# Merging the routing and the expert parts of a small transformer's kernel into one unrolled part

## The chip, the cores and the metric

The kernel runs on one core of a Trainium2 chip. The metric is the device time of one execution in microseconds (us), lower is better. Engines are named as in the profile: PE is TensorE (PEld its weight loads), DVE is VectorE, ACT is ScalarE, POOL is GpSimd, SP is SyncE, which issues the DMAs.

## What is computed

Two layers over x of shape 4 x 1024 x 128 in float32. Each layer is attention and a feed-forward part, each with a layer norm and a modulation (shift, scale, gate) by batch. Only the first layer's feed-forward part matters here. It is a mixture of 16 experts with 64 hidden columns each, and one shared expert:

```python
mod = (silu(L0_c) @ L0_wmod).reshape(4, 6, 1, -1)      # sa, ca, ga, sb, cb, gb
gb = (2 * (gb >= 0) - 1) * maximum(abs(gb), 0.25)
h = layernorm(x) * (1 + cb) + sb
scores = sigmoid(h @ gate_w.T)
# biased = scores + gate_bias; the 2 best of 4 groups of experts stay, of them the 4 best experts;
# weight[token, expert] = scores where chosen, else 0
y = sum_e weight[:, e] * (silu(h @ w1[e].T) * (h @ w3[e].T)) @ w2[e].T
y = y + (silu(h @ ws1.T) * (h @ ws3.T)) @ ws2.T
x = x + gb * y
```

After it come the second layer (windowed attention, then a two-layer local transformer) and the output; the change leaves them alone.

## The kernel before

The token vectors stay in SBUF as X, 32 tiles of 128 tokens, 8 tiles a batch. The program is a sequence of blocks with a barrier between them; in a block each engine runs its own list, tied by semaphores.

**setup** loads constants and computes the modulation. Rows that are multiplied along the free axis are spread over all partitions in rowB (five of them); the gate of the experts, gbT, is kept as a column.

**linear_attention** takes two batches at a time. Each half has two steps of normalisation (ln_stats and ln_apply on DVE, ln_rstd on POOL between them), transposes on PE, the q and v product, a softmax of q on DVE and ACT, and at the end the output products (L463) and the residual on DVE. POOL does only ln_rstd here.

**moe** has two blocks. The first is the routing, a loop over the four batches. A batch is normalised and transposed; ACT writes hT and its rounded copy h_hi, POOL the rest h_lo; PE makes the logits (L565); ACT the exponentials; DVE turns them into scores and compares them pair by pair (wins, gwins, beaten: L629 to L639), makes the weights comb (L662) and splits them into three bfloat16 parts, which PE transposes and ACT stores in combT. The normalisation of the next batch lies between (L166). At the end POOL splits w1 and w3 into two parts each (L555, L556).

The second block is the experts. The 1024 hidden rows and the shared expert's 64 (padded) are nine chunks of 128; the tokens are eight groups of 512. A unit is one chunk of one group, 72 in all. PE makes six up-products of 512 columns in float32r (three for w1, three for w3: L756 to L758, run twice) and a seventh, with sel, that spreads the routing weights of the chunk's two experts over the 128 rows (L760). ACT applies silu (L788), DVE multiplies by the second half (L805) and then by the weights out of PSUM (L808), PE makes the down-product (L746, float32, 512 columns) into one bank. After nine chunks ACT copies the bank with the gate as its scale (yT, L790), PE transposes it back, DVE adds it to X. Two groups are written out, the others run in a loop. A down-product is issued one unit behind its up-products:

```python
                            if j == 1 and not (isinstance(g, int) and g == 0):

                                back(g - 1)
                            if j:
                                down(j - 1)
```

Meanwhile POOL gates the rows of the second layer (L722 to L729).

Of the kernel before, what the change touches and what calls it, by code (L numbers as in the profile page):

```python
# [22 lines left out]
P = 128  # L23
# [3 lines left out]
G4 = 4  # L27
# [62 lines left out]
class Core:  # L90


    L0GA, L1GA, L1SB, L1CB, L1GB = range(5)

    def __init__(self, nc, ctx):
# [10 lines left out]
        self.gbT = sb("gbT", [P, B])  # L106
        self.rowB = sb("rowB", [P, 5, B, D])
# [88 lines left out]
def setup(c, A):  # L196

    nc, X, PS, bank, ident, identb, signal = c.nc, c.X, c.PS, c.bank, c.ident, c.identb, c.counter
    with ExitStack() as sc:
# [9 lines left out]
        gb_abs = ssb("gb_abs", [P, B])  # L209
# [3 lines left out]
        with nc.Block() as block:  # L213
# [30 lines left out]
            def _(dve):  # L244
# [8 lines left out]
                for b in range(B):  # L253
                    dve.tensor_copy(c.rowB[:, 1:5, b, :],
                                    PS[:, b, :].rearrange("p (k d) -> p k d", d=D))
                    last = dve.tensor_copy(c.rowB[:, 0, b, :], PS[:, 4 + b, 0:D])
# [10 lines left out]
                dve.wait_ge(c.act_step.sem, 2)  # L267
                chain(dve.tensor_scalar(c.gbT[:, :], c.modT[:, 0, 5, :], 0.0, 2.0, ALU.is_ge, ALU.mult))
                chain(dve.tensor_scalar(c.gbT[:, :], c.gbT[:, :], 1.0, None, ALU.subtract))
                chain(dve.tensor_tensor(gb_abs[:, :], c.gbT[:, :], c.modT[:, 0, 5, :], ALU.mult))  # L270
                dve.scalar_tensor_tensor(c.gbT[:, :], gb_abs[:, :], 0.25, c.gbT[:, :], ALU.max, ALU.mult)

            @block.tensor
            def _(pe):
                pe.wait_ge(c.dve_step.sem, 2)
                for b in range(B):
                    pe.matmul(PS[:, b, :], csB[:, 1, b, :], wmod[:, 1, 2 * D:6 * D], start=True, stop=True)
                    pe.matmul(PS[:, 4 + b, 0:D], csB[:, 0, b, :], wmod[:, 0, 2 * D:3 * D], start=True, stop=True)
# [7 lines left out]
        c.dve_step.base += 9  # L286

def linear_attention(c, A):

    nc, X, PS, bank, ident, identb, signal = c.nc, c.X, c.PS, c.bank, c.ident, c.identb, c.counter  # L290
    with ExitStack() as sc:
# [31 lines left out]
        with nc.Block() as block:  # L323

            @block.sync
            def _(sp):
                for dst, src in ((wqv[:, :], A["a_wqv"]), (bqv[:, :], A["a_bqv"].partition_broadcast(P)),
                                 (wo[:, :], A["L0_attn_Wo"]), (bo[:, :], A["L0_attn_bo"].partition_broadcast(P)),
                                 (bmask[:, :], A["c_bmask"])):
                    sp.dma_start(dst, src).then_inc(w_loaded.sem, 16)  # L330

            @block.gpsimd
            def _(pool):
                with pool.Fori(0, 2) as bi:
# [3 lines left out]
                    assert chain.k == KP  # L338

# [136 lines left out]
def moe(c, A):  # L476

    nc, X, PS, bank, ident, identb, signal = c.nc, c.X, c.PS, c.bank, c.ident, c.identb, c.counter
    with ExitStack() as mc:
        def msb(name, shape, dt=F32):  # L480
            return mc.enter_context(nc.sbuf_tensor(name, shape, dt))


        h_hi, h_lo = msb("h_hi", [P, NT * P], F32R), msb("h_lo", [P, NT * P], F32R)
        combT = msb("combT", [3 * E, NT * P], BF16)
        w1 = msb("w1", [P, (NJ + 1) * P])
        w3 = msb("w3", [P, (NJ + 1) * P])
        w2 = msb("w2", [P, NJ + 1, D])
        w1_hi, w1_lo, w3_hi, w3_lo = (msb(name, [P, (NJ + 1) * P], F32R) for name in ("w1_hi", "w1_lo", "w3_hi", "w3_lo"))
        sel = msb("sel", [3 * E, NJ, P], BF16)  # L490
        acarrier, pcarrier = msb("acarrier", [P, 1]), msb("pcarrier", [P, 2])
        moe_loaded = signal("moe_loaded")

        with ExitStack() as sc:
            def ssb(name, shape, dt=F32):
                return sc.enter_context(nc.sbuf_tensor(name, shape, dt))

            gw = ssb("gw", [P, E])
            gbias = ssb("gbias", [P, E])
            self32 = ssb("self32", [3 * E, NJ, P])  # L500

            exps = ssb("exps", [P, TB, E])
            score = ssb("score", [P, TB, E])
            biased = ssb("biased", [P, TB, E])
            gmax = ssb("gmax", [P, TB, NG])
            gwins = ssb("gwins", [P, NG, TB, NG], BF16)
            grank = ssb("grank", [P, TB, NG])
            keep = ssb("keep", [P, TB, NG])
            wins = ssb("wins", [P, E, TB, E], BF16)
            beaten = ssb("beaten", [P, E // 2, TB, E], BF16)  # L510
            comb = ssb("comb", [P, TB, E])
            part = ssb("part", [P, TB, P], BF16)
# [186 lines left out]
        with ExitStack() as sc:  # L699
# [15 lines left out]
            with nc.Block() as block:  # L715
# [16 lines left out]
                def _(pe):  # L732
# [8 lines left out]
                    def group(g):  # L741
# [7 lines left out]
                        for j in range(NU):  # L749
# [15 lines left out]
                            if j:  # L765
                                down(j - 1)
# [55 lines left out]

# [1168 lines left out]
```

## Time and profile before

| | |
|---|---|
| Median of three runs | 1713.98 us (1713.75 to 1715.72) |
| The profiled execution | 1710.96 us, of which the span of its instructions is 1709.2 |
| PE, DVE, ACT, POOL busy | 1403.2, 1242.9, 832.5, 620.3 us |
| Linear attention | 23.3 to 122.7 us |
| Routing | 123.4 to 210.5 us |
| Experts | 210.7 to 431.3 us |
| The rest | 431.6 to 1709.2 us |

The stages' bounds are starts and ends of instructions in the timeline. PEclk is the granted clock of TensorE as a share of 2.4 GHz, so 0.50 is 1.2 GHz. A matmul's end is modelled, so it is starts that are to be compared.

### The profile page before, as it was taken

To read this page: it belongs to the slowest core of one execution; us is meant where nothing else is said; L and a number is where in the kernel's file an instruction comes from. 1 tells how busy PE (TensorE), PEld (TensorE's weight loads), DVE (VectorE), ACT (ScalarE), POOL (GpSimd) and SP (SyncE) were. 2 spreads that over 40 slices of the span, in tenths; PEclk is the share of its full clock that TensorE was granted. 3 is DMA by queue.
4 is the path that set the end of the run, shared out by engine and by line. 5 is a ranking of instruction groups with operands and counts; after the bars stand their busy time and mean duration, and the time that the engine had idled before them with its cause. 6 is when DMAs were issued, how large, how long until landed. Compare 5 with 4: busy or idle time off the path is not lost. (4 is left out here: it accounts for less than half of the span.)

```text
span 1709.2 us, 38958 instructions
## 1 busy us (share of the span) xinstructions
PE 1403.2 (82%) x15652; PEld 946.6 (55%) x15652; DVE 1242.9 (73%) x2585; ACT 832.5 (49%) x1677; POOL 620.3 (36%) x494
## 2 busy tenths in 40 slices
PE   4644299999699999994799999967959999998585
PEld 2543155555477777773466666653536666666353
DVE  4669844444478888874899999945459999998354
ACT  1222223232366666662676776632337767765231
POOL 1103430000233334432666566521036666665110
PEclk7775599999699999997999999988989999999798
DMA  2000000000000000002000000001120000000112
GB/s 80 0 14 33 0 0 0 0 0 0 11 8 9 10 9 9 11 10 84 7 14 14 17 14 14 13 14 45 37 65 11 14 17 14 14 17 8 30 49 74
DMA packets 72068, 33.86 MB, mean 20 GB/s; under 512 B 39720, under 2 KB 70192, under 8 KB 71904
## 3 DMA queue, kind: packets, MB, share of 16 engines
q1 hardware_dynamic: 71904, 31.53, 6.7%
q8 instruction: 120, 1.97, 0.5%
q14 instruction: 44, 0.36, 0.1%
HBM read 18.93 MB, written 12.59 MB: 18 GB/s over the span
## 5 line engine op out<-in xcount | busy, mean ns | idle before, releaser
L1444 POOL TENSOR_TENSOR rot<-qk,sinl 128x1024 f32<-128x1024 f32 x64 | 217.5, 3398 | 207.4 <-DVE qk L1494 207.4
L1437 POOL TENSOR_TENSOR rn<-ss,neghalf 128x16 f32<-128x16 f32 x64 | 187.5, 2930 | 67.6 <-DVE ss L1487 60.6
L157 POOL TENSOR_TENSOR vareps<-meanvar,epsv 128x4 f32<-128x4 f32 (+1 forms) x34 | 6.7, 198 | 517.8 <-DVE meanvar L150 286.2
L1618 PE MATMUL PS<-wqkv,hT 128*128 128x512 f32 x256 | 132.2, 640 | 17.6 <-ACT hT L1537 11.0
L1050 DVE TENSOR_REDUCE d_mx<-PS 128x4 f32<-128x576 f32 x128 | 96.9, 757 | 66.0 <-PE PS L1194 63.0
L1542 ACT ACTIVATE qk<-PS 128x512 f32<-128x512 f32 x128 | 76.4, 597 | 138.6 <-PE PS L1618 138.6
L805 DVE TENSOR_TENSOR uu<-sg,PS 128x512 f32<-128x512 f32 x72 | 49.5, 688 | 117.5 <-ACT sg L788 117.5
L1662 PE MATMUL PS<-ident,e_pm 128*128 128x128 f32 x512 | 85.5, 291 | 42.8 <-ACT e_pm L1577 41.2
L1662 PEld LDWEIGHTS PS<-ident,e_pm 128*128 128x128 f32 x512 | 56.3, 145 | 99.8 <-ACT e_pm L1577 90.6
L788 ACT ACTIVATE sg<-PS 128x512 f32<-128x512 f32 x72 | 42.7, 597 | 137.8 <-PE PS L760 123.0
L178 PE MATMUL PS<-ident,xn 128*128 128x128 f32 x132 | 29.3, 366 | 95.5 <-DVE xn L166 74.4
L1113 ACT ACTIVATE pa<-PS 128x512 f32<-128x512 f32 x128 | 76.4, 597 | 61.5 <-PE PS L1203 61.4
L1194 PE MATMUL PS<-kx,d_q 32*64 32x256 f32 (+1 forms) x2048 | 98.0, 306 | 0.0
L1194 PEld LDWEIGHTS PS<-kx,d_q 32*64 32x64 f32 x2048 | 66.4, 133 | 48.6 <-issue 32.7
L1054 DVE TENSOR_TENSOR pm<-PS,d_mx 128x512 f32<-128x512 f32 x128 | 88.5, 691 | 4.4
L1674 PE MATMUL PS<-e_vv,e_pa 128*64 128x65 f32 x2048 | 90.5, 232 | 0.2
L746 PE MATMUL PS<-uu,w 128*128 128x512 f32 x144 | 81.6, 649 | 9.5 <-DVE uu L808 5.1
L1123 ACT ACTIVATE pm<-pm 128x512 f32<-128x512 f32 x128 | 80.6, 630 | 15.1 <-DVE pp L1055 14.6
L1577 ACT ACTIVATE e_pm<-e_pm 128x512 f32<-128x512 f32 x128 | 73.8, 623 | 28.9 <-DVE e_pm L1479 28.9
L756 PE MATMUL PS<-h_hi,w_hi 128*128 (+1 forms) x144 | 86.4, 600 | 1.7 <-DVE carrier L794 1.7
L1475 DVE TENSOR_REDUCE e_mx<-PS 128x8 f32<-128x1024 f32 x64 | 78.4, 1225 | 12.6 <-PE PS L1653 12.5
L1581 ACT ACTIVATE e_pa<-PS 128x512 f32<-128x512 f32 x128 | 76.0, 594 | 23.3 <-PE PS L1662 22.5
(249 smaller groups left out, 3654.8 us busy)
## 6 DMA issues: line engine op xcount, KB each, us to landing
zs<-z_ffn SPq DMA_DIRECT2D x128, 32.0 KB, 1.8
z_attn<-Z SPq DMA_DIRECT2D x64, 64.0 KB, 1.5
zg<-z_attn SPq DMA_DIRECT2D x32, 128.0 KB, 2.4
z_ffn<-Z SPq DMA_DIRECT2D x16, 256.0 KB, 2.3
X<-in_L_attn_x SPq DMA_DIRECT2D x4, 512.0 KB, 6.9
z_ffn<-Z SPq DMA_DIRECT2D x32, 64.0 KB, 1.6
out_x<-X SPq DMA_DIRECT2D x4, 512.0 KB, 3.2
wqkv<-in_e_wqkv SPq DMA_DIRECT2D x2, 768.0 KB, 4.3
```

The costliest lines, as they stand in the source:

```text
L746: return pe.matmul(PS[:, YACC, :], w2[:, j, :], uu[:, j % 2, :], start=(j == 0), stop=(j == NJ))
L756: pe.matmul(PS[:, 3 * p + k, :], hi[:, cols], h_hi[:, tok], start=True, stop=False)
L1050: chain(dve.tensor_reduce(mx[:, par, :, :], s, AX.X, ALU.max))
L1054: dve.tensor_tensor(out, s[:, :, :, 0:2 * W1], bc(mx[:, par, :, :], 3, 2 * W1), ALU.subtract)
L1123: last = act.activation(p, p, ACT.Exp)
L1194: last = pe.matmul(o, q[r:r + 32, b, rows], kk, start=False, stop=True, skip_group_check=True)
L1437: pool.tensor_tensor(rn[:, v % 2, :], ss[:, v % 2, :], c.neghalf[:, :], ALU.pow).then_inc(rn_ready.sem, 1)
L1444: pool.tensor_tensor(rot[:, :, :, :], x, bc(sinl[:, t, :, :], 2, H2), ALU.mult).then_inc(rot_ready.sem, 1)
L1475: steps(dve.tensor_reduce(mx[:, :, :], s, AX.X, ALU.max))
L1618: pe.matmul(c.PS[:, QBANK + s, :], h_of(v), wqkv[:, s * INNER:(s + 1) * INNER], start=True, stop=True).then_inc(eqkv_ready.sem, 1)
L1662: last = pe.transpose(c.PS[:, TBANK, i * P:(i + 1) * P], pm[:, v % 2, h, i // 2, i % 2, :], ident[:, :])
L1674: last = pe.matmul(c.PS[rows, OBANK + h, at * (DH2 + 1):(at + 1) * (DH2 + 1)], pa[:, h, i, rows], vv[:, b, 4 * h + at, (t + 1 + blk) % 2, ...
```

## The change

The two blocks of moe become one, written out without a loop: 72 units in one sequence, with the routing of batches 1 to 3 laid between the units by hand. What else it changes:

- **Routing weights.** They are transposed in float32 (one transpose a batch), copied to SBUF, stored to a DRAM tensor comb_rows by eight DMAs, and loaded back by DMAs that repeat each row over 64 partitions, into cb: two DMAs of 1 MB for each group of 512 tokens, two buffers. POOL multiplies uu by cb. The product with sel and the second DVE product go, and with them the three bfloat16 parts.
- **Scores.** sigmoid is computed as 0.5 tanh(z/2) + 0.5 instead of 1 / (1 + exp(-z)).
- **Order.** The shared expert's chunk comes first in each group. Down-products come two units behind, with four buffers uu.
- **Down-product.** uu is now the stationary operand and w2g the moving one, so four products of 128 columns give tokens on partitions; the transposes back go, and the residual is added from PSUM. w2g is w2 times the gate, for each batch, made on POOL once.
- **Earlier work.** The expert weights are loaded behind linear attention's weights; splitting them, gating the rows and making w2g run on POOL inside linear attention, whose POOL loop is written out. The gate gb becomes a sixth row of rowB, by four more products in setup.

`lead(s, k)` gives the batch whose step k is due at unit s; step k of batch r is at unit 18 r - 26 + k, so that its weights are made 7 units ahead of its first unit.

```diff
+    def split(self, pool):
+        pool.wait_ge(self.loaded.sem, 16 * 5)
+        for k, (w, hi, lo) in enumerate(((self.w1, self.w1_hi, self.w1_lo), (self.w3, self.w3_hi, self.w3_lo))):
+            pool.tensor_copy(hi[:, :], w[:, :]).then_inc(self.w_split.sem, 1)
+            pool.wait_ge(self.w_split.sem, self.w_split.at(2 * k + 1))
+            pool.tensor_tensor(lo[:, :], w[:, :], hi[:, :], ALU.subtract).then_inc(self.w_split.sem, 1)
...
+    def gate_down(self, pool, c):
+        for b in range(B):
+            pool.tensor_tensor(self.w2g[:, b, :, :], self.w2[:, :, :], bc(c.rowB[:, c.L0GB, b, :], 1, NJ + 1), ALU.mult)
...
             @block.gpsimd
             def _(pool):
-                with pool.Fori(0, 2) as bi:
+                for bi in range(2):
                     chain = Chain(pool, c.pool_step, bi * KP)
                     for g in range(2):
                         c.ln_rstd(pool, chain, 4 * bi + 2 * g, G4)
                     assert chain.k == KP
+                    pool.wait_ge(c.xn_ready.sem, c.xn_ready.at(4 * bi + 4))
+                    if bi == 0:
+                        ex.split(pool)
+                        ex.gate_rows(pool, c, (c.L0GB,))
+                        ex.gate_down(pool, c)
+                    else:
+                        one = c.rowB[:, c.L1CB, :, :]
+                        pool.tensor_scalar(one, one, 1.0, None, ALU.add)
+                        ex.gate_rows(pool, c, (c.L1GA, c.L1GB))
...
+                for r in range(B):
+                    sp.wait_ge(combT_ready.sem, combT_ready.at(r + 1))
+                    for t in range(TB):
+                        sp.dma_start(combD[r, t // G4, :, (t % G4) * P:(t % G4 + 1) * P],
+                                     combT[t * E:(t + 1) * E, :]).then_inc(comb_stored.sem, 16)
+                    sp.wait_ge(comb_stored.sem, comb_stored.at(16 * TB * (r + 1)))
+                    for h in range(2):
+                        g = 2 * r + h
+                        if g >= 2:
+                            sp.wait_ge(u_ready.sem, u_ready.at(NJ * (g - 1)))
+                        for half in range(2):
+                            src = combD[r, h, half:E:2, :].partition_broadcast(INTER)
+                            sp.dma_start(cb[half * INTER:(half + 1) * INTER, h, :, :], src).then_inc(comb_loaded[h].sem, 16)
...
+                def weigh(s):
+                    g, k = divmod(s, NU)
+                    if k == 1:
+                        pool.wait_ge(comb_loaded[g % 2].sem, comb_loaded[g % 2].at(32 * (g // 2 + 1)))
+                    if k:
+                        pool.wait_ge(gated.sem, gated.at(s + 1))
+                        pool.tensor_tensor(uu[:, s % 4, :], uu[:, s % 4, :], cb[:, g % 2, ORDER[k], :], ALU.mult)\
+                            .then_inc(u_ready.sem, 1)
...
+                for r in range(2):
+                    rstd(r)
+                    for st in STREAMS:
+                        split_h(r, st)
+                for s in range(NS):
+                    weigh(s)
...
+                def up(s):
+                    g, j = s // NU, ORDER[s % NU]
+                    if s % NU == 0:
+                        pe.wait_ge(h_split.sem, h_split.at(g + 1))
+                    if s >= 2:
+                        pe.wait_ge(gated.sem, gated.at(s - 1))
...
+                def down(s):
...
+                    for i in range(G4):
+                        last = pe.matmul(PS[:, YB + g % 2, i * P:(i + 1) * P], uu[:, s % 4, i * P:(i + 1) * P],
+                                         ex.w2g[:, g // 2, ORDER[k], :], start=(k == 0 and i == 0), stop=True, skip_group_check=(k > 0 or i > 0))
+                    last.then_inc(down_done.sem, 1)
+
+                turn_x(0, 0)
+                turn_x(0, 1)
+                logits(0)
+                for s in range(NS + 2):
+                    if s < NS:
+                        up(s)
+                    if s == 1:
+                        turn_comb(0)
+                        turn_x(1, 0)
+                        turn_x(1, 1)
+                        logits(1)
+                    if s >= 2:
+                        down(s - 2)
...
+                for s in range(NS):
+                    product(s)
+                    if s >= NU and s % NU == 3:
+                        add(s // NU - 1)
...
+                    if lead(s, 11):
+                        scores(lead(s, 11))
+                    if lead(s, 12):
+                        groups()
+                    if lead(s, 13):
+                        kept()
+                    for k in range(4):
+                        if lead(s, 14 + k):
+                            compare(wins, biased, E, range(4 * k, 4 * k + 4))
+                    if lead(s, 18):
+                        count(wins, E, True, True)
+                    if lead(s, 19):
+                        weights(lead(s, 19))
```

`product` is DVE's product of silu and the second half, `compare` a piece of the old pairwise comparison, `count` its sum.

## Rows read from the trace of the kernel before

**Rows 1.** Table of stretches: busy us and instructions by engine, granted clock, DMA.
```profile
core 0: us, PE busy (x) PEld busy (x) DVE busy (x) ACT busy (x) POOL busy (x), PEclk, DMA share, GB/s
123.00:210.50 87.50, 26.79 (x128) 23.08 (x128) 77.68 (x325) 18.61 (x40) 31.30 (x39) 0.51 0.07 23
211.00:216.00 5.00, 5.00 (x11) 3.25 (x12) 0.87 (x2) 3.37 (x4) 4.64 (x3) 0.50 0.00 2
216.00:221.00 5.00, 5.00 (x17) 2.57 (x15) 2.07 (x4) 1.19 (x2) 4.66 (x5) 0.93 0.00 0
211.00:431.30 220.30, 209.32 (x672) 115.67 (x672) 98.10 (x144) 64.37 (x96) 16.48 (x11) 0.96 0.00 0
```

**Rows 2.** Groups by line, 0 to 560 us: busy, mean ns | idle before, releasers.
```profile
L805 DVE TENSOR_TENSOR uu<-sg,PS 128x512 f32<-128x512 f32 x72 | 49.5, 688 | 117.5 <-ACT sg L788 117.5
L788 ACT ACTIVATE sg<-PS 128x512 f32<-128x512 f32 x72 | 42.7, 597 | 137.8 <-PE PS L760 123.0 <-PE PS L758 14.8
...
L788 ACT ACT_TABLE_LOAD x8 | 10.3, 1283 | 0.8 <-ACT gcur L781 0.7
...
L278 PE MATMUL PS<-wmod,csB 128*128 128x128 f32 x8 | 1.9, 322 | 0.0
```

**Rows 3.** Timeline of PE, one unit of the experts: start, us, instruction, count.
```profile
243.05 1.13 PE L746 MATMUL PS<-uu,w 128*128 128x512 f32 x2
...
245.50 0.39 PE L760 MATMUL PS<-combT,sel 48*128 48x512 bf16 x1
245.81 0.70 PE L746 MATMUL PS<-uu,w 128*128 128x512 f32 x1
```

**Rows 4.** Timeline, routing of the first batch, DVE and a DMA issue.
```profile
123.41 1.64 DVE L144 BATCH_NORM_STATS2 stat<-X 128x6 f32<-128x128 f32 x8 [0.67 <-PEq L323]
...
125.15 0.50 SPq L531 DMA_DIRECT2D w<-in_w3T  x1
...
126.86 4.66 DVE L166 TENSOR_SCALAR xn<-X,meanvar,rstd 128x128 f32<-128x128 f32 x8 [1.14 <-POOL rstd L158]
...
136.68 0.95 DVE L648 RECIPROCAL score<-score 128x128 f32<-128x128 f32 x1
...
138.60 2.79 DVE L166 TENSOR_SCALAR xn<-X,meanvar,rstd 128x128 f32<-128x128 f32 x8
...
149.44 0.29 DVE L662 SCALAR_TENSOR_TENSOR comb<-beaten,score 128x128 f32<-128x128 bf16 x1
```

**Rows 5.** Linear attention: waits of its stretch (us, times, longest), and its timeline.
```profile
PE PS L442 <- DVE q L374: 26.5, 4, 7.8
...
67.56 3.84 PE L463 MATMUL PS<-wctx,qT 128*128 128x128 f32 x32
...
76.26 0.20 POOL L157 TENSOR_TENSOR vareps<-meanvar,epsv 128x4 f32<-128x4 f32 x1 [42.01 <-DVE meanvar L150]
```

**Rows 6.** Groups by line of POOL over the whole span.
```profile
L1444 POOL TENSOR_TENSOR rot<-qk,sinl 128x1024 f32<-128x1024 f32 x64 | 217.5, 3398 | 207.4 <-DVE qk L1494 207.4
...
L727 POOL TENSOR_TENSOR rowB<-rowB,l_sgn 128x512 f32<-128x512 f32 x2 | 2.6, 1278 | 0.2
```

**Rows 7.** Timeline of DVE and POOL beside each other, routing of the third batch.
```profile
181.09 2.37 DVE L629 TENSOR_TENSOR wins<-biased 128x120 bf16<-128x120 f32 x2
182.13 1.19 POOL L555 CAST w_hi<-w 128x1152 fp32r<-128x1152 f32 x1
...
183.38 0.18 DVE L632 TENSOR_TENSOR wins<-biased 128x8 bf16<-128x8 f32 x1
183.41 2.61 POOL L556 TENSOR_TENSOR w_lo<-w,w_hi 128x1152 fp32r<-128x1152 f32 x1
183.46 2.68 DVE L629 TENSOR_TENSOR wins<-biased 128x104 bf16<-128x104 f32 x1
```

**Rows 8.** DMA issues: KB of each, median us from issue to landing.
```profile
zs<-z_ffn SPq DMA_DIRECT2D x128, 32.0 KB, 1.8
...
w<-in_w3T SPq DMA_DIRECT2D x1, 576.0 KB, 5.7
...
bqv<-in_a_bqv SPq DMA_DIRECT2D x1, 128.0 KB, 2.7
```

More of the change, by code:

```diff
@@ L90 @@
 class Core:
-    L0GA, L1GA, L1SB, L1CB, L1GB = range(5)
+    L0GA, L1GA, L1SB, L1CB, L1GB, L0GB = range(6)
     def __init__(self, nc, ctx):
@@ L105, in __init__ @@
         self.modT = sb("modT", [P, 2, 6, B])
-        self.gbT = sb("gbT", [P, B])
-        self.rowB = sb("rowB", [P, 5, B, D])
+        self.rowB = sb("rowB", [P, 6, B, D])
         self.PS = ctx.enter_context(nc.psum_tensor("PS", [P, 8, 512], F32))
@@ L255, in _ @@
                                     PS[:, b, :].rearrange("p (k d) -> p k d", d=D))
-                    last = dve.tensor_copy(c.rowB[:, 0, b, :], PS[:, 4 + b, 0:D])
+                    last = dve.tensor_copy(c.rowB[:, 0:c.L0GB + 1:c.L0GB, b, :],
+                                           PS[:, 4 + b, 0:2 * D].rearrange("p (k d) -> p k d", d=D))
                 chain = Chain(dve, c.dve_step, 2)
@@ L265, in _ @@
                                          sgn[:, :, :].rearrange("p a b -> p (a b)"), ALU.max, ALU.mult)
[L267 to L271, printed above, removed]
             @block.tensor
@@ L277, in _ @@
                     pe.matmul(PS[:, b, :], csB[:, 1, b, :], wmod[:, 1, 2 * D:6 * D], start=True, stop=True)
-                    pe.matmul(PS[:, 4 + b, 0:D], csB[:, 0, b, :], wmod[:, 0, 2 * D:3 * D], start=True, stop=True)
+                    for k in range(2):
+                        pe.matmul(PS[:, 4 + b, k * D:(k + 1) * D], csB[:, 0, b, :], wmod[:, 0, (2 + 3 * k) * D:(3 + 3 * k) * D],
+                                  start=True, stop=True)
                 for l in range(2):
@@ new lines, in __init__, with load @@
+        self.loaded, self.w_split, self.gated = c.counter("moe_loaded"), c.counter("w_split"), c.counter("rows_gated")
+    def load(self, sp, A):
+        for dst, src in ((self.w1[:, :], A["w1T"]), (self.w3[:, :], A["w3T"]), (self.w2[:, :, :], A["w2T"]),
+                         (self.gw[:, :], A["gwT"]), (self.gbias[:, :], A["L0_ffn_gate_bias"].partition_broadcast(P))):
+            sp.dma_start(dst, src).then_inc(self.loaded.sem, 16)
+    def split(self, pool):
[4 more added lines that the diff above has]
+            pool.tensor_tensor(lo[:, :], w[:, :], hi[:, :], ALU.subtract).then_inc(self.w_split.sem, 1)
@@ new lines, in gate_rows @@
+    def gate_rows(self, pool, c, rows):
+        step = Steps(pool, self.gated, 5 * (rows[0] != c.L0GB))
+        for row in rows:
+            gate = c.rowB[:, row, :, :]
+            step(pool.tensor_scalar(self.sgn[:, :, :], gate, 0.0, 2.0, ALU.is_ge, ALU.mult))
+            step(pool.tensor_scalar(self.sgn[:, :, :], self.sgn[:, :, :], 1.0, None, ALU.subtract))
+            step(pool.tensor_tensor(gate, gate, self.sgn[:, :, :], ALU.mult))
+            step(pool.tensor_scalar(gate, gate, 0.25, None, ALU.max))
+            step(pool.tensor_tensor(gate, gate, self.sgn[:, :, :], ALU.mult))
@@ L1891, in build @@
         setup(c, A)
-        linear_attention(c, A)
-        moe(c, A)
+        with ExitStack() as mc:
+            ex = Experts(c, mc)
+            linear_attention(c, A, ex)
+            moe(c, A, ex)
         Z = c.sb("Z", [P, NT, D])
```

564 lines of the change are left out of this document (266 added, 298 removed).

## The prediction

> **What bounds the kernel now.** I read the table of stretches first [rows 1]. The routing part (123 to 210.5 us) is VectorE's: 78 us busy of 87.5, TensorE 27, at the lower clock (0.51). The expert part (211 to 431) is TensorE's: 209 busy of 220, VectorE 98, at 0.96. They stand one behind the other, 307.9 us from 123.4 to 431.3, and in each the other engine idles. The groups by line [rows 2] show that in the expert part VectorE waits for ScalarE and ScalarE for TensorE. So a unit (one block of 128 hidden rows for 512 tokens) costs what TensorE needs for it, and the order of TensorE's instructions gives that [rows 3]: from one down-product to the next 2.76 us (243.05 to 245.81). The selection product takes 0.31 (245.50 to 245.81). The down-product has two passes of 512 columns; in [rows 5] a pass of 128 columns with its weight load is 0.12, so I put one of 512 at 0.43 and both at 0.85. What remains is 1.60 for the six up-products and the gaps on both sides.
>
> **Part by part: the unit.** The selection product goes (64 of 72 units). The down-product is turned round: four products with 128 columns and a weight load each, every one in two passes. Their nearest row is that of the last products of linear attention, of the same shape: 32 passes in 3.84 us [rows 5], 0.12 each, so 0.96 for a unit's eight. New unit: 1.60 + 0.96 = 2.56 us. The turning back of the output (yT and its four transposes) goes as well. 72 units are 184.3; the first two up-products run under the routing of batch 0, so 184.3 - 2 x 1.60 = 181.1 us remain. The old stage ran at 0.96 on average, its start at 0.50 included [rows 1]; I take 4% for the same: 7.2.
>
> **The start.** Batch 0 is still routed with nothing beside it. Its weights were ready at 149.44 + 0.29 = 149.7 [rows 4]; between the scores and there, batch 1's normalisation (2.79) and the reciprocal (0.95) disappear: 146.0. TensorE's next units stand behind the turning of these weights and behind batch 1's normalisation, transposes and logits. That same chain ran from 123.41 to about 136.4 in batch 0 of before, with 2.3 lost because the eight xn instructions took 4.66 beside Pool's memsets (now done ahead), so 10.7. Up-product 2 starts at 156.7: 33.3 us after 123.4.
>
> Meanwhile the weights travel: transposed and copied by 147.0, eight stores at 0.45 us an issue to 150.6 (the issue of w3T took 0.50 [rows 4]), landed 1.8 later [rows 8], 152.4; then 2.1 MB for the first group. w1T and w3T, issued right behind each other, 1.15 MB, were there 5.7 after 125.15 [rows 4, 8], so 6.2 after the first issue: 4.4 us beyond a latency of 1.8, 262 GB/s, so 8 + 1.8 us, 162.5 with the issue. With Pool's first product (1.28) that is 163.8; TensorE reaches down-product 1 at 156.7 + 2 x (1.60 + 0.96 + 1.60) = 165.0, at the lower clock. It is just covered. Later loads have a group each (23 us) and are hidden. The Trainium skill (DMA: Bandwidth & Descriptors, Bandwidth, and its rule on two transfers to disjoint partition halves, which run one behind the other) gives 6.15 us for 1 MB; by that estimate a group needs 12.3 and the start comes 3 us later. No row here shows a broadcast of this size.
>
> **Routing inside the stage.** On TensorE batches 2 and 3 add transposes and logits: 16 passes and eight transposes at the 0.12 of [rows 5], 2.9, with short waits 3.6 us each, 7.2; three turnings of weights that wait for VectorE inside the same unit, 1.0 each: 3.0. ScalarE has 0.60 a unit and room for 3.3 us more a batch. Tanh beside Silu may need another table: a load is 1.28 [rows 2], bound 0 to 6; I take 2. (ScalarE: Activation LUTs, in the Trainium skill, section Table sets, lists tanh with exp and with sigmoid and not beside silu; no row here has both.)
>
> Pool now multiplies 128x512 by the weights. The nearest rows are 1.28 us [rows 6], taken while VectorE did expert products, which read one SBUF and one PSUM operand and stayed at 0.69 [rows 2]. The other end is half of rot's 3.40, 1.70. Either fits in 2.56.
>
> But [rows 7] show that VectorE's instructions with two SBUF operands wait while Pool works: two wins instructions took 2.37 us, and the next one 2.68 beside Pool's w_lo of 2.61, where one of the same kind between them took 0.18. In the new stage a unit's routing piece starts when Pool starts on the same unit. So VectorE needs 0.74 + the piece + up to 1.28. Groups, kept, four compares and count are 8.05 us together (141.39 to 149.44 [rows 4]) and go to seven units: 8.05 + 7 x 2.02 - 7 x 2.56 = 4.3 us of lag. The scores (about 0.95, from 137.63 to 138.60) share a unit with a residual add of 0.7: 1.1 more, 5.4 a batch. TensorE asks for a gated product 2.1 us after it is ready in the undisturbed order (0.96 + 1.60 + 0.96 + gaps, less silu and product, 1.4), so 3.3 are paid, three times: 9.9. Bounds 0 (Pool always slips in between) and 24 (double).
>
> The tail (last gating, Pool's product, one down-product, residual add) is 2. Stage: 33.3 + 181.1 + 7.2 + 10.2 + 9.9 + 2 + 2 = 245.7, against 307.9: -62.2.
>
> **What moves into linear attention.** Pool's splitting of w1 and w3 and the gating of rows move from the routing and expert parts to behind the normalisations of attention's two halves, and four products of 128x1152 (2.61 each, as w_lo in [rows 7]) are new. That is about 8 + 8 + 10 = 26 us in the first half and 17 in the second; Pool had 42 us of idleness there before its job at 76.3 [rows 5], so Pool itself is in time. It costs something all the same: VectorE divides q there (0.69), and TensorE waits for it, 26.5 us in all [rows 5]. From then on some ten of VectorE's instructions with two SBUF operands (two divisions, two shifts, two divisions, biases, residuals) meet a Pool that works without a pause, and about five in the second half. By [rows 7] each waits for the rest of Pool's instruction: ten at 0.85 and five at 0.7, 12 us. Bounds: 0, and 20 if most wait for a whole one of 2.6. If the cover failed altogether and Pool were late at 76.3, what is missing would be added one for one.
>
> **Setup.** Four more products, eight passes of 0.32 that overlap in twos [rows 2], 1.3 to 2.6; wider copies and four small instructions less cancel. +1.5. The additional loads stand in SP's queue behind attention's own: nothing.
>
> **Sum.** -62.2 + 12 + 1.5 = -48.7, from the profiled 1710.96: 1662.3. The median shown (1713.98) is 3.0 above that execution; I go part of the way: 1663.
>
> **Rivals.**
> (a) Pool and VectorE do not hurt each other: attention +2 instead of 12, lag 0: about 1643. For it: waits of this kind are seen beside long Pool instructions; rowB's ran beside expert products unharmed. Against it: those have only one SBUF operand. 0.2.
> (b) They hurt twice as much: attention +20 and lag 24: 1663 + 8 + 15 = 1686. For it: the two wins instructions at 181.09 waited for more than one Pool instruction between them. 0.2.
> (c) Slower than before: the broadcast through DRAM bounds. The row of bqv, 128 KB broadcast in 2.7 us [rows 8], allows 48 GB/s if none of it is latency: 43 us a group, eight groups from 152.4 end at about 500, 1663 + 130 = 1793. It decides from 33 us a group (64 GB/s). Against it: zs, 32 KB, takes 1.8, so most of 2.7 is latency. 0.04.
> (d) The clock stays at 1.2 GHz in the merged stage, as in the routing part (0.51), since stalls break TensorE's work: 181 us more, 1844. Against it: at 216 to 221 it was 0.93 five us after a start at 0.50 [rows 1], with the same density. 0.02; a few short falls lie in (b).
> (e) The waiting is as I say but the stage starts later by the loads: +3 to +8, 1669. In my range.
>
> **How the numbers follow.** My case with (e) 0.54, (a) 0.2, (b) 0.2, (c) 0.04, (d) 0.02. The range takes (a) and (b) in and a little of the ends of attention and start: 1636 to 1692. Change within 0.2% is what a measurement can't tell from none; it needs an accident between (b) and (c): 0.01. Faster 0.94, slower 0.05.
>
> **What would show it.** Down-products 2.5 to 2.6 us apart in units without routing; eight passes at 0.12. wins (0.18) and attention's q <- q, rs and q <- q, mx lengthened where Pool is busy; linear attention some 12 us longer. cb's halves landing in 4 to 6 us each; first Pool product near 163 (plus the shift of 13). Pool's product at 1.3. One routing of about 23 us at the start and none later; VectorE behind in units 3 to 11, 21 to 29, 39 to 47. Wrong it would be made above all by the two contention terms and by anything that makes TensorE lose its clock.

## The result

| | before | after |
|---|---|---|
| Median of four runs | 1713.87 us | 1646.33 us (1638.80 to 1655.54) |
| Ratio, 95% interval | | 0.961 (0.958 to 0.964) |
| The profiled execution (span) | 1710.96 (1709.2) | 1645.47 (1643.7) |

Faster by 67.5 us, where 51 were forecast. 1646 lies inside the range (1636 to 1692) and nearer to rival (a), 1643, than to my 1663. By stages, from the starts and ends of instructions in both timelines:

| us | before | forecast | after |
|---|---|---|---|
| Setup, to the first statistics | 23.84 | +1.5 | 24.53 (+0.7) |
| Linear attention | 99.57 | +12 | 102.31 (+2.7) |
| Routing and experts, to the last residual add | 307.9 | 245.7 (-62.2) | 235.0 (-72.9) |
| The rest | 1277.6 | 0 | 1281.5 (+3.9) |

These are two profiles, and code that the change leaves alone differs between profiles too. Linear attention took 99.57, 96.18 and 96.16 us in the three profiles with the old form of it (before and the last two experiments), and 100.1 to 103.6 in the eight with the new form, so the +2.7 of the table is at the low end. The merged part, unchanged in the experiment on attention below, took 232.0 there and 235.0 here. An execution more than 1.5% above the fastest of its kernel, at a lower granted clock, is not compared; only the last merged kernel below has such, two of its four.

First the same table of stretches as [rows 1], now over the merged part: its start, the first load of weights, the remainder, and the two sides of one turning of routing weights.

```profile
core 0: us, PE busy (x) PEld busy (x) DVE busy (x) ACT busy (x) POOL busy (x), PEclk, DMA share, GB/s
126.80:158.70 31.90, 15.41 (x61) 13.16 (x62) 19.16 (x100) 8.82 (x13) 11.80 (x14) 0.56 0.12 27
158.70:171.00 12.30, 6.97 (x29) 5.78 (x30) 2.09 (x5) 1.47 (x3) 3.00 (x3) 0.78 1.05 202
171.00:361.90 190.90, 174.41 (x1021) 151.75 (x1020) 107.36 (x271) 47.14 (x81) 89.23 (x74) 0.95 0.36 73
191.00:196.70 5.70, 1.32 (x11) 1.07 (x10) 5.42 (x23) 0.60 (x1) 2.54 (x2) 0.92 0.00 0
196.70:203.00 6.30, 6.30 (x20) 5.37 (x21) 1.28 (x2) 0.88 (x2) 1.77 (x3) 0.53 0.05 10
```

Nothing in it is VectorE's alone any more except the first routing (19.16 of 31.90) and short pieces like 191.0 to 196.7, where TensorE did 1.32 of 5.70. What TensorE waited for from 169 to 362 (engine, tile, line and releaser: us, times, longest):

```profile
PE PS L658 <- DVE comb L833: 11.4, 3, 4.4
PE PS L684 <- POOL uu L612: 6.3, 2, 5.3
PE PS L670 <- DVE uu L840: 2.2, 7, 0.4
```

TensorE's timeline, one unit, against [rows 3]. A down-product is now eight passes of 128 columns (L684):

```profile
354.80 1.05 PE L684 MATMUL PS<-w2g,uu 128*128 128x128 f32 x8
355.61 0.47 PE L670 MATMUL PS<-h_hi,w_hi 128*128 128x512 f32 x1
```

From the start at 354.80 to the next down-product at 357.08 are 2.28 us, as between the three before it; the down-product holds 0.81 of them (354.80 to 355.61), the six up-products 1.47. Before, a unit was 2.76.

Timeline of the start: the stores of batch 0's weights, the loads, and Pool's first products.

```profile
148.93 3.75 SPq L581 DMA_DIRECT2D comb_rows<-combT  x8
...
153.71 2.98 SPq L590 DMA_DIRECT2D cb<-comb_rows  x4
...
168.00 3.71 POOL L612 TENSOR_TENSOR uu<-uu,cb 128x512 f32<-128x512 f32 x3 [9.51 <-DMA cb<-comb_rows]
...
169.32 2.08 PE L684 MATMUL PS<-w2g,uu 128*128 128x128 f32 x8 [5.33 <-POOL uu L612]
```

TensorE came to down-product 1 at 164.0 and stood 5.33 us. Timeline around the turning of batch 1's weights, which TensorE's list has between two units:

```profile
194.46 0.69 DVE L840 TENSOR_TENSOR uu<-sg,PS 128x512 f32<-128x512 f32 x1
...
196.26 0.37 DVE L833 SCALAR_TENSOR_TENSOR comb<-beaten,score 128x128 f32<-128x128 bf16 x1
...
196.69 0.48 PE L658 MATMUL PS<-ident,comb 128*128 128x128 f32 x1 [4.38 <-DVE comb L833]
...
196.81 0.78 PE L670 MATMUL PS<-h_hi,w_hi 128*128 128x512 f32 x1
```

And groups by line up to 420 us, of Pool's product and of VectorE's instructions that share the stage or attention with Pool:

```profile
L612 POOL TENSOR_TENSOR uu<-uu,cb 128x512 f32<-128x512 f32 x64 | 82.7, 1294 | 108.9 <-DVE uu L840 99.4 <-DMA cb<-comb_rows 9.5
L802 DVE TENSOR_TENSOR wins<-biased 128x120 bf16<-128x120 f32 (+14 forms) x60 | 22.8, 385 | 0.0
L786 DVE TENSOR_SCALAR xn<-X,meanvar,rstd 128x128 f32<-128x128 f32 x32 | 12.1, 439 | 1.5 <-POOL rstd L598 1.2
L379 DVE TENSOR_TENSOR q<-q,rs 128x512 f32<-128x512 f32 x8 | 8.2, 1023 | 0.3
L825 DVE TENSOR_SCALAR grank<-keep 128x32 f32<-128x32 f32 x4 | 4.0, 1000 | 0.1
L391 DVE TENSOR_TENSOR bog<-bo,rowB 128x128 f32<-128x128 f32 x4 | 4.0, 998 | 0.0
```

### The profile page after: what moved, and what is told of

The parts are those of the page before. It is cut to its first block and busy times, and to the rows that moved or that the text cites. A ratio compares the mean times of both kernels' runs of the same rounds, so it can differ in the third digit from the quotient of the medians.

```text
span 1643.7 us, 39262 instructions
## 1 busy us (share of the span) xinstructions
PE 1368.0 (83%) x15968; PEld 978.2 (60%) x15968; DVE 1201.0 (73%) x2487; ACT 807.0 (49%) x1637; POOL 721.5 (44%) x558
## 3 DMA queue, kind: packets, MB, share of 16 engines
q1 hardware_dynamic: 81312, 48.38, 12.1%
## 5 line engine op out<-in xcount | busy, mean ns | idle before, releaser
L1505 POOL TENSOR_TENSOR rot<-qk,sinl 128x1024 f32<-128x1024 f32 x64 | 217.7, 3402 | 209.3 <-DVE qk L1555 209.3
L612 POOL TENSOR_TENSOR uu<-uu,cb 128x512 f32<-128x512 f32 x64 | 82.7, 1294 | 108.9 <-DVE uu L840 99.4
L1642 ACT ACTIVATE e_pa<-PS 128x512 f32<-128x512 f32 x128 | 76.1, 595 | 21.7 <-PE PS L1723 20.7
L684 PEld LDWEIGHTS PS<-w2g,uu 128*128 128x128 f32 x576 | 78.3, 199 | 13.8 <-POOL uu L612 7.5
L1264 PE MATMUL PS<-ident,pm 128*128 128x128 f32 x512 | 80.2, 280 | 7.4 <-ACT pp L1186 7.3
## 6 DMA issues: line engine op xcount, KB each, us to landing
cb<-comb_rows SPq DMA_DIRECT2D x16, 1024.0 KB, 12.1
```

What stands on the lines that cost most here:

```text
L612: pool.tensor_tensor(uu[:, s % 4, :], uu[:, s % 4, :], cb[:, g % 2, ORDER[k], :], ALU.mult)\
L1264: last = pe.transpose(PS[:, TBANK, j * P:(j + 1) * P], pm[:, g % 2, 4 * (j // 2) + 2 * e + j % 2, :], ident[:, :])
L1505: pool.tensor_tensor(rot[:, :, :, :], x, bc(sinl[:, t, :, :], 2, H2), ALU.mult).then_inc(rot_ready.sem, 1)
```

## The experiments

Stage means the merged part, from its first statistics to the end of its last residual add: 235.0 us in the changed kernel (126.84 to 361.88). The kernel before, run beside them, had medians of 1709.26 (first four kernels) and 1710.54 (next four), and 1707.07 in one run beside the last two. A time of one run is named as such: unchanged code after the stage took from 1276.6 to 1295.7 us in these profiles, so single runs are read by their stage. The stage itself is sure to some 3 us only (235.0 and 232.0 with the same code).

**The turning, with later place.** Every routing step comes two units earlier, and only the turning of the weights on TensorE (and the copy on ScalarE) keeps its unit, so it stands two units behind the weights.

```diff
-    LEAD = 8
+    LEAD = 10
...
-                    if lead(s, 19):
-                        turn_comb(lead(s, 19))
+                    if lead(s, 21):
+                        turn_comb(lead(s, 21))
...
-                    if lead(s, 19):
-                        take_comb(lead(s, 19))
+                    if lead(s, 21):
+                        take_comb(lead(s, 21))
```

> The changed kernel with every routing step of batches 1 to 3 two units earlier and the turning of the weights (PE) and its copy (ACT) two units later against the rest, so PE finds comb ready. The merged part took 235.0 us (126.84 to 361.9). Theory A (the stall is the place of the turning in PE's list: 11.4 us of waiting for comb, and the clock falls to 0.50 behind each of the three, some 3 us each): 215 us. Theory B (VectorE is too far behind because of Pool, and PE would then wait for gated products instead): 11 us of the waiting come back at PE's up-products, 228 us or more.

Measured: stage 221.5 (128.71 to 350.18), 1633.05 us, ratio 0.9548 (0.953 to 0.9565); between the 215 and the 228 of the two theories. TensorE's waits from 172 to 350:

```profile
PE PS L670 <- DVE uu L840: 5.3, 12, 1.1
...
PE PS L684 <- POOL uu L612: 2.6, 3, 1.0
```

The three waits for comb are gone; 13.5 us came back, more than the 11.4 waited, although waits for gated products grew from 2.2 to 5.3. Behind a wait TensorE had run at 0.53 (the row of 196.7 to 203.0), its up-products 0.43 us apart (197.81 to 198.24) where a unit at full clock has 0.23. That is 6.3 x 0.47, about 3 us lost behind a wait of 4.4. The down-products on both sides say the same: 12.00 us for two units (191.25 to 203.25), of which 4.56 are the units, 4.38 the wait and 0.12 the turning. Behind the other two turnings it is 1.7 (245.14 to 255.89, wait 4.38) and 1.8 (297.78 to 306.92, wait 2.67). The balance of this run fits: 13.5 - 11.4, less 1.2 for a shorter wait for the first load (4.1 instead of 5.3), with 3.1 and 1.6 of new waits, leaves 5.6 for three, 1.9 each. The granted clock was 0.99 from 172.0 to the stage's end, where it had been 0.95.

**Without Pool's product.** Pool waits for the same things, but writes one column of another tile; the weighting is left out.

```diff
-                        pool.tensor_tensor(uu[:, s % 4, :], uu[:, s % 4, :], cb[:, g % 2, ORDER[k], :], ALU.mult)\
-                            .then_inc(u_ready.sem, 1)
+                        pool.memset(marks[:, s:s + 1], 0.0).then_inc(u_ready.sem, 1)
```

> The changed kernel; Pool's product with the routing weights is left out, a memset of one column signals in its place, and all loads and waits stay. Theory A (Pool's reads hold VectorE up, which makes comb late): wins falls from a mean of 385 ns to its 290, gwins from 449 to 170, grank from 1000 to 180; the wait for comb from 11.4 to under 3 us; the part 12 to 18 us shorter. Theory B (VectorE's routing pieces are late by their own length, Pool is innocent): means unchanged, the part within 4 us of 235.

Measured: stage 217.7, so 17.3 less; 1643.12 in one run, with 1295.7 behind the stage (its windowed attention took 384.7 instead of 370.2; the cause is open). Groups by line:

```profile
L802 DVE TENSOR_TENSOR wins<-biased 128x120 bf16<-128x120 f32 (+14 forms) x60 | 12.9, 221 | 0.0
L786 DVE TENSOR_SCALAR xn<-X,meanvar,rstd 128x128 f32<-128x128 f32 x32 | 8.9, 342 | 1.3 <-POOL rstd L599 1.0
...
L825 DVE TENSOR_SCALAR grank<-keep 128x32 f32<-128x32 f32 x4 | 0.7, 181 | 0.1
```

**Pool busy as long, but reading nothing.** The product is replaced by a memset of 128x1408, which takes nearly the product's time; again the weighting is left out.

```diff
-                        pool.tensor_tensor(uu[:, s % 4, :], uu[:, s % 4, :], cb[:, g % 2, ORDER[k], :], ALU.mult)\
-                            .then_inc(u_ready.sem, 1)
+                        if s > 1:
+                            pool.wait_ge(u_ready.sem, u_ready.at(NJ * g + k - 1))
+                        pool.memset(marks[:, :], 0.0).then_inc(u_ready.sem, 1)
```

> As the run without Pool's product, but Pool writes a scratch tile for about as long (1.3 us) in place of the product: Pool as busy, reading nothing. Theory A1 (only Pool's reads hold up an instruction with two SBUF operands): wins and gwins as without the product, xn and grank may stay long. Theory A2 (any Pool instruction holds VectorE up): wins near 385, the part near 235 us.

Measured: stage 222.9, 1632.52 in one run. Groups by line:

```profile
L615 POOL MEMSET marks<- 128x1408 f32 x64 | 81.5, 1274 | 98.0 <-DVE uu L842 85.0 <-DMA cb<-comb_rows 12.6
L804 DVE TENSOR_TENSOR wins<-biased 128x120 bf16<-128x120 f32 (+14 forms) x60 | 12.9, 221 | 0.0
L788 DVE TENSOR_SCALAR xn<-X,meanvar,rstd 128x128 f32<-128x128 f32 x32 | 11.8, 547 | 1.6 <-POOL rstd L599 1.3
...
L827 DVE TENSOR_SCALAR grank<-keep 128x32 f32<-128x32 f32 x4 | 3.9, 977 | 0.1
```

Two kinds come apart. The comparisons (two SBUF inputs) are free, 221 ns, as soon as Pool doesn't read; grank and xn (one SBUF input and a scalar) stay slow, 977 and 547. So it is not Pool's being busy that holds the first kind. The Trainium skill (SBUF — State Buffer, section "SBUF: two separate sides") says so: an instruction of VectorE with two SBUF inputs is kept out only by a GpSimd instruction that reads SBUF, one in a 2-port mode by any. The comparisons agree with it, 385 beside reading and 221 beside writing; grank and xn agree if they run in such a mode, which no run here shows. Of the 17.3 us, 12.1 go with Pool's reading and 5.2 with its being busy. About 2.5 of the 5.2 are Pool's own instruction in the chain: at the start TensorE stood 3.9 instead of 5.2 for it, at the end VectorE 1.41 instead of 2.58. The remaining 2.7 are within the 3 us by which the stage varies, so that holding grank and xn costs time is not shown. TensorE's waits for comb are 7.3 in both runs, where under 3 had been expected of the first: even with the comparisons undisturbed, VectorE's list was too long for that place.

**Attention without Pool's reading work.** Splitting, gating of rows and w2g are left out and their tiles filled by memsets.

```diff
-                        ex.split(pool)
-                        ex.gate_rows(pool, c, (c.L0GB,))
-                        ex.gate_down(pool, c)
...
+                        pool.wait_ge(ex.loaded.sem, 16 * 5)
+                        for t in (ex.w1_hi, ex.w1_lo, ex.w3_hi, ex.w3_lo):
+                            pool.memset(t[:, :].bitcast(F32), 0.01)
+                        pool.memset(ex.w2g[:, :, :, :], 0.01)
```

> The changed kernel without Pool's reading work in linear attention: splitting w1 and w3, gating the rows and w2g are left out (memsets fill the tiles), so the numbers of later layers are wrong in value only. Theory A (Pool's reads lengthen q <- q, rs from 692 to 1023 ns, bog from 281 to 998): both back at 692 and 281, and the merged part begins 2.5 to 3.5 us earlier than 126.84. Rival (the later begin comes from setup and from 1.7 MB of loads behind attention's own): begins within 0.7 us of 126.84.

Measured: linear attention 98.3 (23.61 to 121.91), with the work 102.3; 1637.82 in one run. The stage begins 4.9 us earlier, 0.9 of them in setup. Groups by line:

```profile
L376 DVE TENSOR_TENSOR q<-q,rs 128x512 f32<-128x512 f32 x8 | 5.5, 692 | 0.3
...
L388 DVE TENSOR_TENSOR bog<-bo,rowB 128x128 f32<-128x128 f32 x4 | 1.1, 282 | 0.0
```

The contention costs attention 4.0 us in this pair of profiles, and 1.8 to 5.3 against the eight profiles with the work (100.1 to 103.6). That VectorE is held is sure (1023 against 692 ns, 998 against 282); the price is known only so far. In the changed kernel's timeline one sees why not 12:

```profile
44.71 0.69 DVE L379 TENSOR_TENSOR q<-q,rs 128x512 f32<-128x512 f32 x1
44.78 3.11 POOL L509 TENSOR_TENSOR w_lo<-w,w_hi 128x1152 fp32r<-128x1152 f32 x1
...
46.62 1.83 DVE L379 TENSOR_TENSOR q<-q,rs 128x512 f32<-128x512 f32 x1
...
60.57 11.22 POOL L523 TENSOR_TENSOR w2g<-w,rowB 128x1152 f32<-128x1152 f32 x4
...
62.26 1.83 DVE L379 TENSOR_TENSOR q<-q,rs 128x512 f32<-128x512 f32 x1
...
69.66 2.29 DVE L391 TENSOR_TENSOR bog<-bo,rowB 128x128 f32<-128x128 f32 x1
```

At 44.71 VectorE was first, and Pool's subtraction took 3.11 instead of 2.62. Only VectorE's instructions that start while one of Pool's runs have to wait, and those are few: two divisions at 1.83, two bog (1.14, 2.29). In the changed kernel q<-q,rs, q<-q,mx and bog are some 6 us longer in all. When the residual adds came (from 71.98), Pool had finished: the four adds of X with bog stand at 0.69.

**First group in two parts.** The first two chunks of group 0 are loaded by DMAs of their own, 256 KB each, with their own semaphore; the other six follow in 768 KB.

```diff
+                            if g == 0:
+                                src = combD[r, h, half:half + 4:2, :].partition_broadcast(INTER)
+                                sp.dma_start(cb[half * INTER:(half + 1) * INTER, h, 0:2, :], src).then_inc(comb_first.sem, 16)
...
-                    if k == 1:
+                    if s == 1:
+                        pool.wait_ge(comb_first.sem, comb_first.at(32))
+                    if k == (3 if g == 0 else 1):
```

> The changed kernel with the first group's two 1 MB loads of weights cut into four: the first two chunks (2 x 256 KB) come first with a semaphore of their own. Pool then waited 9.5 us for the load, PE 5.3 for Pool, and the clock was at 0.50 for the 5 us behind it. Theory A (the start is held by the size of the load, some 200 GB/s): PE's wait for Pool goes, and the merged part takes 235.0 - 5.3 - 2.5 = 227 us. Theory B (it is held by a fixed latency, stores and issue): Pool's wait shrinks by less than 3 us and the part takes 232 or more.

Measured: stage 228.2 (126.84 to 355.00), 6.8 less; 1638.94 in one run. TensorE's wait for Pool there fell from 5.3 to 0.2 (both lists have 1.0 more, at the stage's end). The other 1.7 fit the clock behind it: in the changed kernel it was 0.50 from 169.3 to 175.0, with TensorE busy for 5.68 of the 5.70 us, and here 1.00 from 163 to 173. DMA issues (KB of each, median us from issue to landing):

```profile
cb<-comb_rows SPq DMA_DIRECT2D x14, 1024.0 KB, 12.1
cb<-comb_rows SPq DMA_DIRECT2D x2, 768.0 KB, 10.2
comb_rows<-combT SPq DMA_DIRECT2D x32, 8.0 KB, 1.4
cb<-comb_rows SPq DMA_DIRECT2D x2, 256.0 KB, 4.5
```

**Both edits together**, the later turning and the split load, as shown above.

> Later turning (part 221.5 us) and the first load cut in one kernel. If the two stalls are independent: 221.5 - 7.8 = 214 us, execution about 1625 us. If PE only waits elsewhere: over 219.

Measured: stage 216.4, 1624.31 us, ratio 0.9505 (0.9477 to 0.9532). 13.5 and 6.8 would add up to 214.7, which the stage's 3 us don't tell from 216.4. Pool waits 8.1 us for loads now, where the split load alone had 4.3.

**Both, and the product shared.** In the units in which VectorE has routing work with two SBUF inputs, VectorE multiplies by cb itself, behind its own product: its instructions run in order and can't collide with each other. 23 units of 64.

```diff
+        def by_dve(s):
+            return s >= 6 and s % NU != 0 and (any(lead(s, k) for k in range(11, 20)) or any(lead(s, k) not in (None, 1) for k in (3, 4)))
...
+                    if by_dve(s):
+                        g, k = divmod(s, NU)
+                        dve.wait_ge(comb_loaded[g % 2].sem, comb_loaded[g % 2].at(32 * (g // 2 + 1)))
+                        dve.wait_ge(gated.sem, gated.at(s + 1))
+                        dve.tensor_tensor(uu[:, s % 4, :], uu[:, s % 4, :], cb[:, g % 2, ORDER[k], :], ALU.mult)\
+                            .then_inc(u_dve.sem, 1)
```

> As both together, and the product with the weights is VectorE's in the units that carry a piece of contended routing (steps 3, 4 and 11 to 19, from unit 6 on), Pool's in the others. Theory A (the shared port makes VectorE late: 0.74 + piece + 1.28 against 2.28 a unit; now 0.74 + piece + 0.69): wins back near 290 or below, PE's 8 us of waiting for gated products and Pool's go to under 3, the part 6 to 8 us shorter than with both: 207. Rival (what is left is VectorE's own length): no gain, 213 or more.

Measured: stage 210.9 (207 if contention was what made VectorE late, 213 or more if not, had been expected), 1620.64 us, ratio 0.9476 (0.9442 to 0.9511). Stretch of the stage, and groups by line:

```profile
core 0: us, PE busy (x) PEld busy (x) DVE busy (x) ACT busy (x) POOL busy (x), PEclk, DMA share, GB/s
126.70:337.60 210.90, 187.56 (x1108) 163.80 (x1108) 124.18 (x399) 57.44 (x97) 73.87 (x67) 0.92 0.41 82
```

```profile
L914 DVE TENSOR_TENSOR uu<-uu,cb 128x512 f32<-128x512 f32 x23 | 15.9, 691 | 0.7
L827 DVE TENSOR_TENSOR wins<-biased 128x120 bf16<-128x120 f32 (+14 forms) x60 | 14.8, 252 | 0.0
```

VectorE took over 15.9 us of products, and is busy less than with both edits alone (124.2 against 129.6), since comparisons fell from 454 to 252 ns. In the profiles the stage is 5.5 shorter than with both edits alone; the whole times overlap (1615.49 to 1627.39, and 1622.37 to 1630.86), so the gain is likely and not shown. It has the lowest median of this study.

**One unit earlier still**, otherwise the same:

```diff
-    LEAD = 10
+    LEAD = 11
```

> As the shared product, with the routing steps one more unit ahead (11 for 8 at first), so that the loads of batches 1 to 3 have a unit more. In the run with the later turning Pool waited 3.5 us for a load. Part 2 us shorter than the shared product: 205, if that wait is on PE's path; same if it is hidden.

Measured: stage 209.4; 1619.92 and 1620.58 us, and two runs of 1645.57 and 1649.2. The first two lie inside the range of the shared product (1615.49 to 1627.39), and the stage is 1.5 shorter: no gain is shown.

**Kernel before, with the down-product turned alone.** Four products with uu stationary into the bank; what follows is unchanged, so what is added to X is not turned rightly.

```diff
-                            return pe.matmul(PS[:, YACC, :], w2[:, j, :], uu[:, j % 2, :],
-                                             start=(j == 0), stop=(j == NJ))
+                            for i in range(G4):
+                                last = pe.matmul(PS[:, YACC, i * P:(i + 1) * P], uu[:, j % 2, i * P:(i + 1) * P], w2[:, j, :],
+                                                 start=(j == 0 and i == 0), stop=True, skip_group_check=(j > 0 or i > 0))
```

> The kernel before with the down-product alone turned round (uu stationary, w2 moving, four products of 128 columns; the copy and the transposes behind it stay, so they turn the wrong way and the output's values mean nothing). The prediction's prices: 0.85 out, 0.96 in, a unit 2.76 + 0.11 = 2.87 us, the experts' part 8 us longer than 220.3. The changed kernel's pace (down-product to next up-product 0.81): 2.72 and 3 us shorter. If the gaps between the products go with the old form too: 2.6, 10 us shorter.

Measured: 1710.12 in one run. Timeline of TensorE:

```profile
245.03 1.16 PE L747 MATMUL PS<-w,uu 128*128 128x128 f32 x8
245.94 0.48 PE L758 MATMUL PS<-h_hi,w_hi 128*128 128x512 f32 x1
...
247.51 0.39 PE L762 MATMUL PS<-combT,sel 48*128 48x512 bf16 x1
247.82 1.16 PE L747 MATMUL PS<-w,uu 128*128 128x128 f32 x8
```

A unit is 2.79 (245.03 to 247.82) against 2.76: turning the product neither costs nor saves by itself. The expert part took 220.8 us (207.16 to 427.99), against 220.3 (210.99 to 431.31), so neither the 8 longer nor the 3 or 10 shorter that had been expected.

**Kernel before, without the selection product.** VectorE's second product takes another bank; the weighting is left out.

```diff
-                            if j < NJ:
-                                last = pe.matmul(PS[:, 3 * p + 2, :], sel[:, j, :], combT[:, tok], start=True, stop=True)
...
-                                last = dve.tensor_tensor(uu[:, p, :], uu[:, p, :], PS[:, 3 * p + 2, :], ALU.mult)
+                                last = dve.tensor_tensor(uu[:, p, :], uu[:, p, :], PS[:, 3 * p + 1, :], ALU.mult)
```

> The kernel before with the selection product left out (VectorE's second product reads the up-product's bank in its place, so the weights are left out). The prediction's price: 0.31 a unit, 64 units: 2.45 a unit and 20 us less of 220.3. If the product also brings a gap of its own in front (0.09 to 0.12): 2.35 and 27 us less.

Measured: 1683.45 in one run; the expert part is 23.6 us shorter (196.7 instead of 220.3). Timeline of TensorE:

```profile
245.10 1.13 PE L746 MATMUL PS<-uu,w 128*128 128x512 f32 x2
...
247.45 1.02 PE L746 MATMUL PS<-uu,w 128*128 128x512 f32 x2
```

This unit is 2.35 (245.10 to 247.45), its neighbours on both sides 2.29, and so it alternates. The selection product cost 0.41 to 0.47 a unit, not the 0.31 between its start and the next instruction's: with it goes a gap of 0.1 in front. The kernel before shows it by itself, in the unit of the shared expert, which has no selection product:

```profile
233.87 1.13 PE L746 MATMUL PS<-uu,w 128*128 128x512 f32 x2
...
236.22 1.02 PE L746 MATMUL PS<-uu,w 128*128 128x512 f32 x2
```

From 233.87 to 236.22 are 2.35 us too.

## Why the prediction came out as it did

Direction, mechanism and range held: the routing of batches 1 to 3 did vanish under TensorE's units, Pool was in time, the clock held, and one unit costs what TensorE's order gives. The forecast was 17 us too high: 10.7 in the stage, 9.3 in attention, 0.8 in setup, less the 3.9 by which the rest grew. In the stage there is some luck: the unit was 20 us too dear, and the turnings (8.4) and the first load (5.3), too cheap, hid a good part of that, while the waits for gated products were 7.7 too dear. The merged stage, term by term (the last column from the rows above; the clock is an estimate, the share of the clock that was missing times TensorE's busy time):

| us | forecast | measured |
|---|---|---|
| Start, to up-product 2 | 33.3 | 31.9 (126.84 to 158.72) |
| Units, less the first two's up-products | 181.1 (2.56 each) | 72 x 2.28 - 2 x 1.47 = 161.2 |
| Waits for the first load | 0 | 5.3 |
| Waits at the three turnings | 3.0 | 11.4 |
| Waits for gated products | 9.9 | 2.2 |
| Clock below full | 7.2 | 0.22 x 7.0 + 0.05 x 174.4 = 10.2 |
| Routing of batches 2 and 3 on TensorE, tables, tail, and what I can't assign | 7.2 + 2 + 2 = 11.2 | 12.8 |

**The unit (-20 us) is the step that failed in size.** "What remains is 1.60 for the six up-products and the gaps on both sides" left a gap of the selection product in the price of the new unit, and 0.96 for the down-product came from passes of the same shape elsewhere, 0.12 each, which are 0.10 here. So 0.13 and 0.15 us a unit were too much. The runs: 2.76, less 0.41 to 0.47 (no selection product), plus 0.03 (turned), is 2.32 to 2.38. The changed kernel has 2.28. Up to 0.10 remains, and is seen in the down-product, 0.81 against 0.91 in the old order (245.03 to 245.94). What of the new order gives it (operands ready long before, the two units of distance) was not told apart. The trace before had the first part of it: the shared expert's unit of 2.35 priced the selection product at 0.41.

**The start.** Up-product 2 came 31.9 us in, 1.4 earlier than forecast. "It is just covered" was wrong by 5.3, from both sides. TensorE came to down-product 1 37.2 us in (164.0), and not 41.6: its up-products followed each other by 0.43 us up to 161.4 and by 0.23 from 162.7, and from up-product 2 to there were 5.3 us, where I had 8.3, all at the lower clock. Pool's first product was done 42.5 us in (169.3), and not 40.4. 4.4 and 2.1, less the 1.2 that the sum had to spare, are the 5.3. The loads were issued 2.1 earlier than forecast (153.7, 26.9 in) but took 14.3 us to Pool's start: they moved 202 GB/s (158.7 to 171.0, DMA share 1.05) and not the 262 GB/s that I took from w1T and w3T. From 153.7 to 168.0 186 GB/s moved, 2.7 MB where the group has 2.1: by this estimate part of the second group's loads, issued right behind, went before the first group's end. The estimate by the Trainium skill (DMA: Bandwidth & Descriptors, Bandwidth), which stood beside the sum, put the start 3 us later; here TensorE's wait alone was 5.3. That the wait was for bytes is shown by the split load: the wait went, and the stage was 6.8 us shorter.

**The turnings.** I had priced each at 1.0 and put the lag into waits for gated products. Together my terms were 12.9, and 13.6 were waited, but in another place: in TensorE's list the turning stands in front of all later units, so VectorE's whole lag of a batch is paid there, in one piece (4.4, 4.4 and 2.7 us), and the clock behind it too. That is what the first experiment gives back. The 2.2 for gated products is low: a unit in which TensorE waited 0.30 for one is 2.85 long (242.29 to 245.14), 0.57 more than the others.

**Contention in the stage** was read rightly as a mechanism: comparisons 385 against 221 ns. I had counted only instructions with two SBUF operands; grank (1000 against 181), and xn wait too.

**Attention.** "Some ten of VectorE's instructions meet a Pool that works without a pause, and about five in the second half", at 0.7 to 0.85 each, made 12; the contention costs 4.0 in one pair of profiles, 1.8 to 5.3 over all. An instruction that starts first makes Pool wait instead, Pool's pauses let some through, and the residual adds came after Pool's end. Against the old form (99.57 in the profile before, 96.2 in two others) the changed attention is 2.7 to 6.2 us longer; that the written-out loop of Pool has a part in this is neither shown nor excluded.

**Table loads.** None was added: one load in the stage, 1.28 us, and tanh and silu alternate after it with none. The Trainium skill (ScalarE: Activation LUTs, Table sets) doesn't show the two in one set; here they need no reload. Of my 2 us nothing was due.

**Setup** cost 0.7 where I had 1.5 (24.3 to 25.7 in the profiles of the changed form with all its work, 23.4 to 23.8 before).

**The rest** took 3.9 us more in code that the change leaves alone. The windowed attention is equal (370.8 and 370.2); the local transformer took 896.0 before and 900.5 after, and in the other profiles anything from 895.1 to 902.4, with the same instructions. The cause is open. It means that differences of 3 us between whole times are not read as effects here, nor are such differences between stages.

**Rivals.** (a), no contention, gave nearly the time for the wrong reason: contention is there (12 us of the stage, in one profile) and the cheaper units outweigh it. (b) fell: attention +2.7, not +20. (c) fell: a load takes 12.1 us in the median and the first group 14.3, not 33. (d) fell: granted clock 0.95 from 171 to 362. (e) came true in its condition, with 5.3 us of waiting for the loads, and was outweighed by the unit.

## What to carry to other kernels

In a list that runs in order, the place of an instruction that waits is decided by when its producer is done in the worst case, not by when its result is needed: moved two units behind its producer, this one gave 13.5 us. The price of a small instruction is the unit's length with and without it, gap included. Where two engines hinder each other, try giving the work to the one that would be held, for just the stretches in which it has such work (5.5 us less in the stage here), and let the first consumer of a long load wait for its own part of it.

## What the runs showed of the hardware

- VectorE's comparisons of two SBUF operands took 385 ns beside Pool's product of two SBUF operands, and 221 beside a memset by Pool of equal length; its instructions with one SBUF operand and a scalar were held by both (grank 1000 and 977 ns, alone 181; xn 439 and 547, alone 342). The hold goes both ways: Pool's 2.62 us subtraction took 3.11 when VectorE was first.
- After 4.4 us of waiting at 191 to 196.7 the granted clock was 0.53 for the next 6.3 us, the lower level (1.2 GHz) nearly throughout, with TensorE busy all the time; it had been 0.92. What followed cost about 3 us more; behind the two other waits of the kind (4.4 and 2.7 us) it was 1.7 and 1.8.
- Loads that repeat rows of 2 KB over 64 partitions ran at 202 GB/s, with all DMA engines busy; the first four of 1 MB, issued together, landed 9.0 to 21.7 us after their issue, all sixteen 12.1 in the median, and two of 256 KB in front 4.5.
- Eight passes of 128 columns with four different stationary tiles took 0.81 us in one order of the list and 0.91 in another.
